# Handing out the delta rule's dot products in steps of one feature

## The reference, cut to what matters

```python
hk = concat([relu(hk), relu(-hk)]);  hq = concat([relu(hq), relu(-hq)])      # 128 values per head
hk = concat([hk * roll(hk, 1), hk * roll(hk, 2)]);  hq likewise               # 256 features
hk = hk / hk.sum(-1);  hq = hq / hq.sum(-1)
denom_acc = cumsum(hk, over the sequence)
# scan over the sequence: v_old = k_t . W;  new_v = b_t * (v_t - v_old);  W += k_t x new_v;  out_t = q_t . W
out = SCALE * out / (denominator + EPS)
```

## Time and profile before

| | |
|---|---|
| runs of the kernel, us | 3721.92, 3723.31, 3731.75 (median 3723.31) |
| the profiled execution, us | 3721.55, with a span of 3719.6 |
| TensorE busy | 2784.2 us, 75% of the span |
| VectorE busy | 2052.8 us, 55% |
| ScalarE busy | 1359.4 us, 37% |
| GpSimd busy | 897.8 us, 24% |
| costliest group | L2349, the dots stage's feature products, 369.0 us |
| first and last start of L2349 | 2535.1 and 3151.0 us |

### The profile page before, as it was taken

The page is one execution under the profiler, slowest core; times in us unless marked ns, Lnnn a source line. Parts: engine busy times, 40 slices in busy tenths (PEclk is TensorE's granted clock), DMA queues, the critical chain, the costliest instruction groups (busy, mean ns, idle before and its releaser), DMA issues. The chain is left out here.

```text
span 3719.6 us, 31897 instructions
## 1 busy us (share of the span) xinstructions
PE 2784.2 (75%) x10138; PEld 1394.3 (37%) x10146; DVE 2052.8 (55%) x3662; ACT 1359.4 (37%) x1980; POOL 897.8 (24%) x608
## 2 busy tenths in 40 slices
PE   2006898999999889999777867937888888287317
PEld 1003444555555534444344442423222222055303
DVE  7997432222222465655544476126766666587687
ACT  1003433111111256666434311415666666243003
POOL 0003565000000000000122402133777777200004
PEclk6558999999999999999778879979999999599558
DMA  2001121000000275455100020120000000100001
GB/s 50 0 0 46 46 62 47 0 0 0 0 0 0 49 139 146 138 147 139 32 1 1 1 71 20 57 58 30 1 1 2 7 1 0 31 1 1 2 0 29
DMA packets 107447, 125.99 MB, mean 34 GB/s; under 512 B 22283, under 2 KB 60300, under 8 KB 107052
## 3 DMA queue, kind: packets, MB, share of 16 engines
q1 hardware_dynamic: 105260, 120.13, 12.4%
q0 software_dynamic: 2048, 4.20, 0.4%
HBM read 108.55 MB, written 14.16 MB: 33 GB/s over the span
## 5 line engine op out<-in xcount | busy, mean ns | idle before, releaser
L2349 PE MATMUL dots_x<-all_xt,delta_wE 128*128 128x512 f32 x768 | 369.0, 614 | 70.1 <-DVE dots_g L2465 68.6
L2332 POOL TENSOR_TENSOR dots_pr<-dots_g 128x1536 f32<-128x1536 f32 (+2 forms) x98 | 296.1, 3043 | 143.6 <-DVE dots_g L2465 119.1
L1012 DVE SCALAR_TENSOR_TENSOR attn_sim<-attn_sc,attn_mask 128x512 f32<-128x512 f32 (+3 forms) x256 | 125.8, 491 | 316.9 <-PE attn_sc L938 313.8
L938 PE MATMUL attn_sc<-attn_q,attn_xb 128*128 128x512 f32 (+3 forms) x768 | 295.0, 486 | 0.0
L949 PE MATMUL attn_op<-attn_sim,attn_v 128*128 128x512 f32 (+3 forms) x768 | 295.0, 486 | 0.0
L2462 DVE TENSOR_TENSOR dots_m<-dots_x,dots_sg 128x512 f32<-128x512 f32 x256 | 170.3, 685 | 213.0 <-ACT dots_sg L2384 124.7
L1298 DVE TENSOR_TENSOR grp_h<-grp_sq,grp_cb 128x512 f32<-128x512 f32 x256 | 176.5, 692 | 192.1 <-ACT grp_sq L1186 171.8
L1126 PE MATMUL grp_po<-grp_h,grp_down 128*128 128x512 f32 x512 | 266.4, 602 | 6.0 <-DVE grp_h L1298 6.0
L1118 PE MATMUL grp_ph<-all_xt,grp_up 128*128 128x512 f32 x512 | 263.9, 598 | 0.5 <-ACT grp_sg L1202 0.5
L2349 PEld LDWEIGHTS dots_x<-all_xt,delta_wE 128*128 128x128 f32 x768 | 134.6, 190 | 304.6 <-issue 160.8
L1180 ACT ACTIVATE grp_r<-grp_ph 128x512 f32<-128x512 f32 x272 | 162.4, 597 | 185.5 <-PE grp_ph L1118 183.8
(11 more groups left out here) (614 smaller groups left out, 4961.9 us busy)
## 6 DMA issues: line engine op xcount, KB each, us to landing
grp_cb<-grp_combine SPq DMA_DIRECT2D x512, 128.0 KB, 3.2
mix_cb<-top_weights SPq DMA_DIRECT2D x64, 256.0 KB, 3.2
cap_xs<-cap_zero SPq DMA_DIRECT2D x7, 320.0 KB, 4.4
experts_xe<-cap_xs SPq DMA_DIRECT2D x7, 320.0 KB, 3.4
all_x<-in_L_attn_x_dram SPq DMA_DIRECT2D x4, 512.0 KB, 5.2
cap_w<-in_L_ffn_W_dram SPq DMA_DIRECT2D x1, 2048.0 KB
cap_ys<-experts_yo SPq DMA_DIRECT2D x8, 256.0 KB, 2.3
delta_h<-all_xn SPq DMA_DIRECT2D x1, 2048.0 KB
```

Of the source, the lines that this page charges most:

```text
L938: nc.tensor.matmul(sc[k % SC][:, 0:w], xb[:, m * P:(m + 1) * P], q[:, par, n0:n0 + w], start=True, stop=True).then_inc(s_mm, 1)
L2332: nc.gpsimd.tensor_tensor(slot[w % SLOTS][:, at:at + n], a_, b_, ALU.mult).then_inc(pool_ready, 1)
L2349: nc.tensor.matmul(bank(n, sh)[:], wE[:, 1 - k % 2, a, sh], XTj[:, k // 2, par::2], start=True, stop=True).then_inc(u_mm, 1)
```

## The change

It replaces the orders written out by hand with one order of STEPS = 137 steps. In step n every engine first does its part of feature n (ScalarE: its sign), and then the units that fall due for it; a unit is due two thirds of a step after the one before it, with an offset of its own for VectorE, ScalarE and TensorE. So TensorE alternates one feature with two units and one feature with one unit. The order of the 12 units in a chunk is another, so that GpSimd's come every second. A unit waits only for the features that it reads (NEEDS), which lets GpSimd start a chunk after its fifth feature. ScalarE's "abs" units of chunk 0 also wait for the transfer that saves the tensor in which two of the slots lie, and the middle sums_out is moved behind the first unit of chunk 8. No arithmetic is added or removed.

```diff
--- before.py
+++ after.py
@@ -2289,8 +2289,10 @@
             SLOTS = 5
             OWN = SLOTS - 2
             PIECES = (((0, 1, 4),), ((0, 5, 3), (3, 7, 1)), ((1, 3, 4),), ((1, 7, 1), (2, 5, 3)))
-            UNITS = [("abs", 0, 0), ("abs", 1, 0), ("pool", 0, 0), ("dve", 2, 0), ("pool", 1, 0), ("pool", 3, 0),
-                     ("abs", 0, 1), ("pool", 0, 1), ("dve", 2, 1), ("abs", 1, 1), ("pool", 1, 1), ("pool", 3, 1)]
+            NEEDS = (5, 8, 7, 8)
+            DVE_AFTER, ACT_AFTER, PE_AFTER = 16, 22, 24
+            UNITS = [("pool", 0, 0), ("abs", 0, 0), ("pool", 0, 1), ("dve", 2, 0), ("pool", 1, 0), ("abs", 1, 0),
+                     ("pool", 3, 0), ("abs", 0, 1), ("pool", 1, 1), ("dve", 2, 1), ("pool", 3, 1), ("abs", 1, 1)]
             NU = len(UNITS)
             made_by = {kind: [i for i, u in enumerate(UNITS) if u[0] == kind] for kind in ("pool", "dve")}
             pool_upto = [sum(len(PIECES[u[1]]) for u in UNITS[:i + 1] if u[0] == "pool") for i in range(NU)]
@@ -2315,15 +2317,26 @@
                 s_, a0, n = PIECES[u][piece]
                 return g[:, I % 2, sh, a0:a0 + n], g[:, I % 2, sh, 2 * s_:2 * s_ + 1].to_broadcast([P, n, GROUP]), n
 
+            NFEAT, NUNIT = NI * NF, NI * NU
+            STEPS = NFEAT + NF + 1
+
+            def features_needed(w):
+                I, pos = divmod(w, NU)
+                kind, u, _ = UNITS[pos]
+                return NF * I + (NF - 1 + u if kind == "abs" else NEEDS[u])
+
+            def due(n, offset):
+                return [w for w in range(NUNIT) if (2 * w + offset) // 3 == n]
+
             with nc.Block() as block:
 
                 @block.gpsimd
                 def _(pool):
                     pool.wait_ge(h_out, 16)
                     for I in range(NI):
-                        pool.wait_ge(g_ready, NF * (I + 1))
                         for pos in made_by["pool"]:
                             w = I * NU + pos
+                            pool.wait_ge(g_ready, features_needed(w))
                             if w >= SLOTS:
                                 pool.wait_ge(unit_mm, w - SLOTS + 1)
                             at = 0
@@ -2334,10 +2347,8 @@
 
                 @block.tensor
                 def _(pe):
-                    def feature(I, k):
-                        if I >= NI:
-                            return
-                        n = I * NF + k
+                    def feature(n):
+                        I, k = divmod(n, NF)
                         par, a = divmod(I, NCH)
                         for sh in range(SHIFTS):
                             before, kind = divmod(SHIFTS * n + sh - XB, SHIFTS)
@@ -2348,8 +2359,8 @@
                                     pe.wait_ge(m_ready, 2 * before + kind)
                             nc.tensor.matmul(bank(n, sh)[:], wE[:, 1 - k % 2, a, sh], XTj[:, k // 2, par::2], start=True, stop=True).then_inc(u_mm, 1)
 
-                    def unit(I, pos):
-                        w = I * NU + pos
+                    def unit(w):
+                        I, pos = divmod(w, NU)
                         par, a = divmod(I, NCH)
                         kind, u, sh = UNITS[pos]
                         g_, b_ = (u, 2) if kind == "abs" else divmod(u, 2)
@@ -2363,34 +2374,30 @@
                         ins.then_inc(unit_mm, 1)
 
                     pe.wait_ge(sel_made, 3)
-                    for k in range(NF):
-                        feature(0, k)
-                    for I in range(NI):
-                        for q in range(4):
-                            feature(I + 1, 2 * q)
-                            feature(I + 1, 2 * q + 1)
-                            for pos in range(3 * q, 3 * q + 3):
-                                unit(I, pos)
+                    for n in range(STEPS):
+                        if n < NFEAT:
+                            feature(n)
+                        for w in due(n, PE_AFTER):
+                            unit(w)
 
                 @block.scalar
                 def _(act):
-                    def sign(I, k):
-                        if I >= NI:
-                            return
-                        n = I * NF + k
+                    def sign(n):
                         act.wait_ge(u_mm, SHIFTS * n + 1)
                         if n >= 2:
                             act.wait_ge(m_ready, 2 * (n - 1))
                         nc.scalar.activation(sg[:, n % 2], bank(n, 0)[:], ACT.Sign).then_inc(sg_ready, 1)
 
-                    def unit(I, pos):
-                        w = I * NU + pos
+                    def unit(w):
+                        I, pos = divmod(w, NU)
                         kind, u, sh = UNITS[pos]
                         v_ = slot[w % SLOTS]
                         if kind == "abs":
-                            act.wait_ge(g_ready, NF * (I + 1))
+                            act.wait_ge(g_ready, features_needed(w))
                             if w >= SLOTS:
                                 act.wait_ge(unit_mm, w - SLOTS + 1)
+                            if I == 0:
+                                act.wait_ge(h_out, 16)
                             nc.scalar.activation(v_, g[:, I % 2, sh, u::2], ACT.Abs).then_inc(unit_ready, 1)
                             return
                         if kind == "pool":
@@ -2407,28 +2414,13 @@
                         for k in range(3):
                             nc.scalar.activation(ev[:, k], sums[k][:], ACT.Copy).then_inc(ev_ready, 1)
 
-                    for k in range(NF):
-                        sign(0, k)
-                    for I in range(NI):
-                        if I == NCH:
-                            sums_out(0)
-                        unit(I, 0)
-                        sign(I + 1, 0)
-                        unit(I, 1)
-                        sign(I + 1, 1)
-                        for pos in (2, 3, 4):
-                            unit(I, pos)
-                        sign(I + 1, 2)
-                        sign(I + 1, 3)
-                        for pos in (5, 6, 7):
-                            unit(I, pos)
-                        sign(I + 1, 4)
-                        sign(I + 1, 5)
-                        for pos in (8, 9, 10):
-                            unit(I, pos)
-                        sign(I + 1, 6)
-                        unit(I, 11)
-                        sign(I + 1, 7)
+                    for n in range(STEPS):
+                        if n < NFEAT:
+                            sign(n)
+                        for w in due(n, ACT_AFTER):
+                            unit(w)
+                            if w == NCH * NU:
+                                sums_out(0)
                     sums_out(1)
 
                 @block.sync
@@ -2465,26 +2455,22 @@
                             ins = stt(g[:, I % 2, sh - 1, k], m[:, n % 2, sh - 1], 0.0, bank(n, 0)[:], ALU.max, ALU.mult)
                         ins.then_inc(g_ready, 1)
 
-                    def products(I, pos):
-                        w = I * NU + pos
-                        dve.wait_ge(g_ready, NF * (I + 1))
+                    def products(w):
+                        I, pos = divmod(w, NU)
+                        dve.wait_ge(g_ready, features_needed(w))
                         if w >= SLOTS:
                             dve.wait_ge(unit_mm, w - SLOTS + 1)
                         if I == 0:
                             dve.wait_ge(h_out, 16)
-                        a_, b_, n = factors(I, pos, 0)
+                        a_, b_, _ = factors(I, pos, 0)
                         tt(slot[w % SLOTS], a_, b_, ALU.mult).then_inc(dve_ready, 1)
 
-                    for k in range(NF):
-                        feature(0, k)
-                    for I in range(NI):
-                        feature(I + 1, 0)
-                        products(I, made_by["dve"][0])
-                        for k in range(1, 5):
-                            feature(I + 1, k)
-                        products(I, made_by["dve"][1])
-                        for k in range(5, NF):
-                            feature(I + 1, k)
+                    for n in range(STEPS):
+                        if n < NFEAT:
+                            feature(n)
+                        for w in due(n, DVE_AFTER):
+                            if w % NU in made_by["dve"]:
+                                products(w)
 
         alpha = s.sb("alpha", [P, len(PAIRS), P])
         with Stage(nc, "alg") as s1:
```

## The result

The changed kernel takes 3632.52 us (median of 4 runs, 3626.2 to 3635.22) against 3727.53 us for the kernel before (4 runs, 3721.92 to 3734.82). The ratio is 0.9739, 95% interval 0.9725 to 0.9753. The forecast was 3629 us. The profiled executions took 3721.55 and 3632.42 us, 89.1 us apart.

The account below looks back on a forecast made before the run. It took the stage to be bound by a loop of waits, with no engine full. Fifteen chunks at 33.6 instead of 39.42 us save 87, the end 7: 94 us off 3721.55 gives 3627.5, median 3629 us, range 3610 to 3682.

Parts of the forecast that it names:

- TensorE's sum per step: TensorE's features and units: 4.63 us for a step with two units, 3.75 with one, 33.5 a chunk.
- Case A: The forecast itself: TensorE sets the pace, 33.6 us a chunk, 3629 us in all; chance 0.66.
- The feature loop: TensorE's third product, VectorE's feature work and back: 0.65 us of room in a short step, 1.5 in a long one.
- ScalarE's margin: Unit made in the step that sums it: ready at T + 3.52, wanted at T + 3.66 (T: step's start); costed at nothing.
- The race after feature 7: VectorE's first product and GpSimd's unit 4 both follow feature 7; VectorE should be first, its product taking about 2.3 us.
- the second product: VectorE's second product of a chunk: waits 0.7 us for GpSimd's one-feature piece, about 2.9 us in all.
- rival B: GpSimd wins the race after feature 7 or still runs unit 2: 2.8 us a chunk, 3671 us in all; chance 0.12.
- GpSimd's early start: GpSimd's unit 0 may start once feature 4 is done, at 21.6 us of the chunk; laid out from 24.0 to 28.5.
- The end: Last feature to the sums' copy: 27.8 us against 34.9 before, 7 us less, between 3 and 10.
- The whole: Fifteen chunks 39.42 - 33.6 shorter, 87 us, plus 7 at the end: 94 us less, 3629 us.
- the late signs of rows 4: ScalarE's signs queued behind two relus of 1.9 us hold TensorE's features, giving gaps of 1.36 and 0.26 us.
- Rival E: Five slots: units just miss their step, each slot's life grows to 18.2 us, 43.7 a chunk, 3780 us; chance 0.05.

Follow-up runs that it names:

- Experiment 4: Changed kernel with ScalarE's offset 24 instead of 22, so it makes its part of a unit in the step that sums it; 3815.19 us, ratio 1.0164 to the kernel before.
- Experiment 10: Changed kernel plus a VectorE sum over m, about 1.1 us, just ahead of each chunk's first product; 3697.63 us, ratio 0.9905 to the kernel before.
- experiment 6: Changed kernel with GpSimd and VectorE's products waiting for all eight features of a chunk; 3811.81 us, ratio 1.0154 to the kernel before.
- needs_only, experiment 2: Kernel before with one edit: each GpSimd unit waits only for the features it reads, all orders old; 3715.53 us, ratio 0.996.
- experiment 7: Changed kernel with TensorE and ScalarE taking two steps at a time, ScalarE's lead of one unit kept; 3729.98 us, ratio 1.0002 to the kernel before.
- experiment 11: Changed kernel with four slots instead of five; 3636.01 us, ratio 0.9745 to the kernel before.
- experiment 9: Changed kernel plus a VectorE memset of 1024 columns just ahead of each chunk's first product; 3666.24 us, ratio 0.9775 to the kernel before.

## Why the prediction was right

- TensorE's sum per step (4.63, 3.75) and per chunk (33.5, taken as 33.6): measured 4.63 and 33.58. Case A held to the number.
- The feature loop and ScalarE's margin, 0.14 us for a unit made in its own step: costed at nothing, and rightly: VectorE never waits for a sign in the stage, and TensorE never idles in the chunk. The unit that ScalarE makes from 2760.30 to 2762.21 is summed from 2762.29, 0.08 us later. Experiment 4 takes the lead from the other units too, and the chunk is 44.06.
- The race after feature 7: VectorE first, as forecast, 2.28 us in every chunk; the second product 2.78 (about 2.9 forecast). Experiment 10 put rival B's price at 36.38, forecast 36.4, and added 1.6 for the clock where it fell.
- GpSimd's early start: unit 0 can come before feature 7 and does; experiment 6 took that away and lost 10 us a chunk.
- The end: 28.6 us, 27.8 forecast.
- The whole: 94 us less forecast, 89.1 between the profiled executions, 95.0 between the medians (90.8 from the median of the three runs before that the forecast knew). The stage itself gave 94.5, and the stages ahead of it another 3.1. What is missing went in the stage "out", the same code: 183.4 us at a clock of 0.92 in the one profile of before, 190.6 at 0.90 after. In the profiles of the twelve experiments it took from 186.2 to 192.1 us, needs_only, the closest to the old kernel, being the longest. So it looks like scatter of that stage and not like a price of the change, though the kernel before has only its one profile.
- Wrong in the reasoning, though not in the sum: I read the late signs of rows 4 as the cause of the gaps, the one of 1.36 us included. VectorE's rows behind the held product of the kernel before, and TensorE's next gap:

```profile
2768.80 1.27 DVE L2462 TENSOR_TENSOR dots_m<-dots_x,dots_sg 128x512 f32<-128x512 f32 x2
2769.99 1.27 DVE L2465 SCALAR_TENSOR_TENSOR dots_g<-dots_m,dots_x 128x512 f32<-128x512 f32 x2
2773.14 1.29 DVE L2462 TENSOR_TENSOR dots_m<-dots_x,dots_sg 128x512 f32<-128x512 f32 x2 [1.87 <-ACT dots_sg L2384]
...
2775.67 1.13 PE L2349 MATMUL dots_x<-all_xt,delta_wE 128*128 128x512 f32 x2 [1.51 <-DVE dots_g L2465]
```

  The feature that ends the gap of 1.36 us follows the product without waiting for a sign; this gap is the hold itself. The gap of 1.51 us ends with a feature whose sign was late, and that sign stood behind the relu of the same held product.
- What the change brings: in the new order, ScalarE's lead of one unit, GpSimd's early start and the steps of one feature are each needed; experiments 4, 6 and 7 each take one away and each gives back the whole gain. A first product that is not held is worth 2.8 us a chunk of it (experiment 10), or 4.4 where the clock falls. How the old order's 5.84 us a chunk divide is shown only in part: by experiment 2 the first product's hold of 4.80 - 2.28 = 2.5 us goes almost whole into the chunk, so some 2.5 us are my estimate for it. For the rest no run adds the lead or the new order of units alone to the old kernel, so it stays open.
- Rival E's fixed life of a slot: refuted by experiment 11.

## What to carry to other kernels

When engines hand work round in a loop, write down for each unit when it is ready and when it is wanted, and give the maker a lead; the queue position named by the longest wait may be only where the wait shows. Parts of such a schedule do not add up: 0.8 us alone, 10 in company. Here a VectorE instruction with two SBUF inputs, placed right behind the event that also releases GpSimd, took its own time only (2.28 us), and GpSimd paid 2.1 us for it; caught behind a running GpSimd instruction it took 3.97 to 5.88 us (experiments 2, 7 and 10).

## What the runs showed of the hardware

- A lead of 0.08 us by the records' starts did not decide for GpSimd: its record was first and GpSimd waited (experiment 9, the memset). With 0.97 us GpSimd kept its place (10). The Trainium skill ("SBUF — State Buffer", section "Who interferes with whom") gives the ports that the two engines share to whoever issues first, for the whole instruction; the runs agree for 0.97 us and not for 0.08 by the records' starts; a record's start may not be the moment of issue.
- A VectorE memset of 1024 fp32 columns kept GpSimd's multiplication waiting (3.0 us more in experiment 9 with the product's 2.2 in it); a reduction with one SBUF input did not (10: 6.75 us for the pair, as with the product alone).
- TensorE idle for 2.5 to 2.7 us between matrix products was in some chunks followed by products at about half speed (24 records in 4.48 us instead of 2.78, experiment 7), which cost 1.6 to 1.7 us on top of the gap; the granted clock in the middle of these records (2775.15 to 2777.15) was 0.50, the lower of the two levels (1.2 GHz). In the next chunk of the same run the same gap of 2.72 us had no such fall behind it.
